# Scan loop of a fused MetaFormer kernel: PSUM places by first release, 14 slots, y summed five tiles behind the scan, GpSimd's u four tiles ahead, weighing by pairs of tiles

## What is computed

```python
def _mamba(x, in_w, conv_w, conv_b, x_w, dt_w, dt_b, A_log, D, out_w):
    ...
    xc = jax.nn.silu(jnp.transpose(xt, (0, 2, 1)))
    dbl = xc @ x_w.T
    dt, Bm, Cm = jnp.split(dbl, [DT_RANK, DT_RANK + D_STATE], axis=-1)
    dt = jax.nn.softplus(dt @ dt_w.T + dt_b)
    A = -jnp.exp(A_log)
    dA = jnp.exp(dt[..., None] * A)
    dBx = dt[..., None] * Bm[:, :, None, :] * xc[..., None]
    def step(h, inp):
        dA_t, dBx_t, C_t = inp
        h = dA_t * h + dBx_t
        y = jnp.einsum('bds,bs->bd', h, C_t)
        return (h, y)
    ...
    y = jnp.swapaxes(ys, 0, 1) + xc * D
    y = y * jax.nn.silu(z)
    return y @ out_w.T
```

## Time and profile before

| what | value |
|---|---|
| three runs | 901.69, 905.27, 906.05 us (median 905.27) |
| the profiled execution | 901.04 us, of which the span from first to last instruction is 899.3 us |
| scan loop, first POOL operation to last gate | 302.07 to 804.71 us |
| busy over the span | PE 708.9, DVE 721.3, POOL 516.2, ACT 369.3 us |
| DMA | 102.81 MB, 36.6% of the 16 engines for the main queue |

### The profile page before, as it was taken

One profiled execution on the slowest core, in us unless ns is written; L12 is line 12 of the kernel. 1 busy time (PEld: TensorE's weight loads), 2 busy tenths in 40 slices (PEclk: granted clock), 3 DMA queues, 4 the chain that ended last, 5 costly groups with the idle time before them and its releaser, 6 DMA issues. The chain is left out here.

```text
span 899.3 us, 19137 instructions
## 1 busy us (share of the span) xinstructions
PE 708.9 (79%) x7722; PEld 442.3 (49%) x7722; DVE 721.3 (80%) x938; ACT 369.3 (41%) x585; POOL 516.2 (57%) x407
## 2 busy tenths in 40 slices
PE   7987886699877387788878878887887787787696
PEld 3554553356554154544544544454454454446363
DVE  3998887763320489999999989999999999974998
ACT  2220002156536755545555555555455554321000
POOL 5000000000010489999999999999999999970043
PEclk9999998889989799999999999999999999998799
DMA  4000000000004256666666665666667666600001
GB/s 162 5 4 4 5 4 2 3 1 1 1 1 126 74 171 210 197 187 190 212 194 188 197 203 177 189 209 196 189 189 213 187 198 205 195 30 1 0 12 41
DMA packets 55866, 102.81 MB, mean 114 GB/s; under 512 B 11169, under 2 KB 13345, under 8 KB 55777
## 3 DMA queue, kind: packets, MB, share of 16 engines
q1 hardware_dynamic: 55552, 100.73, 36.6%
q0 software_dynamic: 224, 0.85, 0.2%
HBM read 98.00 MB, written 3.54 MB: 113 GB/s over the span
## 5 line engine op out<-in xcount | busy, mean ns | idle before, releaser
L546 POOL TENSOR_TENSOR ring<-ring,big 128x576 f32<-128x576 f32 x206 | 285.1, 1406 | 13.7 <-DVE ring L936 11.8
L184 PE MATMUL banks<-ring,main_params 128*128 128x288 f32 x824 | 244.2, 426 | 4.6 <-POOL ring L546 2.8
L936 DVE TENSOR_TENSOR_SCAN ring<-big,banks 128x576 f32<-128x576 f32 x154 | 202.6, 1340 | 2.3
L184 PEld LDWEIGHTS banks<-ring,main_params 128*128 128x128 f32 x824 | 146.4, 192 | 60.0 <-POOL ring L546 15.7
L924 DVE TENSOR_TENSOR banks<-banks,big 128x576 f32<-128x576 f32 x192 | 143.0, 745 | 24.0 <-PE banks L1218 21.4
L718 ACT ACTIVATE big<-big,small 128x576 f32<-128x576 f32 x192 | 142.2, 764 | 27.3 <-DVE ring L936 21.5
L523 POOL COPY big<-normed 128x288 f32<-128x288 f32 x8 | 3.0, 429 | 244.2 <-DVE normed L422 244.2
L1217 PE MATMUL banks<-big,selectors 96*128 96x512 bf16 x192 | 74.5, 390 | 80.0 <-DVE ring L936 37.4
L356 PE MATMUL banks<-big 32*32 32x288 f32 x3712 | 96.9, 429 | 21.3 <-issue 17.2
L790 DVE SCALAR_TENSOR_TENSOR big<-big 128x288 f32<-128x288 f32 x216 | 93.6, 512 | 0.0
L718 ACT ACTIVATE banks<-big,small 128x576 f32<-128x576 f32 x64 | 47.4, 741 | 108.2 <-DVE ring L936 86.9
(11 more groups left out here) (166 smaller groups left out, 962.5 us busy)
## 6 DMA issues: line engine op xcount, KB each, us to landing
big<-bc_rows SPq DMA_DIRECT2D x640, 144.0 KB, 3.2
bc_rows<-big SPq DMA_DIRECT2D x16, 144.0 KB, 2.4
residual<-x_in SPq DMA_DIRECT2D x2, 576.0 KB, 5.8
out<-big SPq DMA_DIRECT2D x2, 512.0 KB, 3.0
main_params<-main_in SPq DMA_DIRECT2D x1, 895.0 KB, 8.7
big<-front_in POOLq DMA_DIRECT2D x1, 574.5 KB, 5.7
experts<-experts_in SPq DMA_DIRECT2D x1, 512.0 KB, 9.0
row_selectors<-rows_in POOLq DMA_DIRECT2D x1, 256.0 KB, 5.9
```

The lines of the kernel that those rows point to most:

```text
L184: last = nc.tensor.matmul(PS[rows, 2 * p + a, 0:HALF], lhsT, rhs[:, bass.ds(at + a * HALF, HALF)], start=start, stop=stop, skip_group_chec ...
L546: nc.gpsimd.tensor_tensor(slot, slot, CT[n % 10], ALU.mult).then_inc(weighted, 1)
L936: nc.vector.tensor_tensor_scan(slot, DECAY[m % 3], place, 0.0, ALU.mult, ALU.add).then_inc(scanned, 1)
```

## The change

- A PSUM place goes to the user whose predecessor is released first by a small table of due times (`released`), instead of going round by three. bc stands behind tile 7 instead of 9.
- Two more pairs of slots, in the tensor XN, make 14 instead of 10. Slots come in pairs that lie side by side.
- POOL weighs two tiles in one operation of 1152 columns, and C is loaded for two tiles by one DMA per direction (five buffers of double width).
- POOL makes u four tiles ahead instead of two.
- PE adds y five tiles behind the scan instead of three, by a new list `ADDS`; the gate stands behind scan 5 instead of scan 3.
- A DVE multiply is put off by one tile where its place is released late (`late`), tiles 2, 8 and 9 instead of 2 and 10.

```diff
-        CT = [big(L) for _ in range(10)]
+        CT = [big(2 * L) for _ in range(5)]
...
-        MORE = [big(L) for _ in range(2)]
+        MORE = big(2 * L)
...
-        SLOT = [RING[:, i * L:(i + 1) * L] for i in range(8)] + MORE
+        SLOT_PAIR = ([RING[:, 2 * i * L:2 * (i + 1) * L] for i in range(4)] + [MORE] +
+                     [XN[:, 2 * i * L:2 * (i + 1) * L] for i in range(2)])
+        PAIRS = len(SLOT_PAIR)
+        SLOT = [t[:, i * L:(i + 1) * L] for t in SLOT_PAIR for i in range(2)]
...
-        V_AFTER, BC_AFTER = 1, 9
-        AHEAD = 2
+        V_AFTER, BC_AFTER = 1, 7
+        AHEAD, POOL_AHEAD = 2, 4
...
+        def released(user):
+
+            kind, i = user
+            if kind == "tile":
+                return i + 1
+            return (i - PREPARED) * DS + (V_AFTER if kind == "v" else BC_AFTER + 1.2)
+
+        HELD, PLACES, OWNER_AHEAD = [None] * 3, {}, {}
+        for user in USERS:
+            place = min(range(3), key=lambda p: -1 if HELD[p] is None else released(HELD[p]))
+            PLACES[user], OWNER_AHEAD[user] = place, HELD[place]
+            HELD[place] = user
...
+        def late(n):
+
+            owner = OWNER_AHEAD["tile", n]
+            return owner is not None and released(owner) > n - 1.4
...
-            for n in range(NTILES):
-                b, s = n // DS, n % DS
-                if s == 0:
-                    sp.wait_ge(rows_stored[b % 3], 16 * (b // 3 + 1))
-                if n >= 10:
-                    sp.wait_ge(weighted, n - 9)
-                spread_row(CT[n % 10], b, 1, s, c_loaded[n % 10])
...
+            for n in range(-POOL_AHEAD, NTILES):
+                m = n + POOL_AHEAD
+                if m < NTILES and m % DS == 0:
+                    sp.wait_ge(rows_stored[m // DS % 3], 16 * (m // DS // 3 + 1))
+                if m in POOL_TILES:
+                    load_b(m)
+                if n >= 0 and n % 2 == 0:
+                    load_c(n // 2)
...
-            def weigh(n):
-                pool.wait_ge(scanned, n + 1)
-                pool.wait_ge(c_loaded[n % 10], 32 * (n // 10 + 1))
-                slot = SLOT[n % SLOTS]
-                nc.gpsimd.tensor_tensor(slot, slot, CT[n % 10], ALU.mult).then_inc(weighted, 1)
+            def weigh(k):
+
+                pool.wait_ge(scanned, 2 * k + 2)
+                pool.wait_ge(c_loaded[k % 5], 32 * (k // 5 + 1))
+                slots = SLOT_PAIR[k % PAIRS]
+                nc.gpsimd.tensor_tensor(slots, slots, CT[k % 5], ALU.mult).then_inc(weighted, 1)
...
-            LATE = [V_AFTER + 1, BC_AFTER + 1]
             for n in range(-AHEAD, NTILES):
+                if n == 10:
+                    dve.wait_ge(z_mm, 2 * J)
                 if n >= 0:
                     scan(n)
                 for m in (n + 1, n + 2):
-                    if m in DVE_TILES and m - (1 if m % DS in LATE else 2) == n:
+                    if m in DVE_TILES and m - (1 if late(m) else 2) == n:
                         inputs_on_dve(m)
-                if n >= DS and n % DS == 3:
+                if n >= DS and n % DS == 5:
                     gate_image(n // DS - 1)
...
-                pe.wait_ge(weighted, n + 1)
+                pe.wait_ge(weighted, n // 2 + 1)
...
-            ADDS = [[-3], [-2], [-1], [], [0], [1, 2]] + [[s - 3] for s in range(6, DS)]
-            for n in range(-AHEAD, NTILES + 3):
+            ADDS = [[-5], [-4], [-3], [-2], [-1], [], [0], [1], [2, 3], [4]] + [[s - 5] for s in range(10, DS)]
+            for n in range(-AHEAD, NTILES + 5):
```

More of the change, by code:

```diff
@@ L220, in build_program @@
         rows_stored = [sem(f"rows_stored{i}") for i in range(3)]
-        c_loaded = [sem(f"c_loaded{i}") for i in range(10)]
+        c_loaded = [sem(f"c_loaded{i}") for i in range(5)]
         b_loaded = [sem(f"b_loaded{i}") for i in range(3)]
@@ L470, in store_rows, with spread_rows, load_b, load_c @@
                 sp.dma_start(BCD[b].rearrange("w d s t -> (w d s) t"), STAGE[b % 3]).then_inc(rows_stored[b % 3], 16)
[L472 removed]
+            def spread_rows(dst, b, w, s, count, loaded):
                 for d in range(2):
[L475 to L476 removed]
+                    rows = BCD[b, w, d, s:s + count].rearrange("s t -> (s t)")
+                    sp.dma_start(dst[d * DI:(d + 1) * DI, :], rows.unsqueeze(0).to_broadcast([DI, count * L])).then_inc(loaded, 16)
+            def load_b(n):
+                m = POOL_TILES.index(n)
+                if m >= 3:
+                    sp.wait_ge(u_pool, m - 2)
+                spread_rows(BT[m % 3], n // DS, 0, n % DS, 1, b_loaded[m % 3])
+            def load_c(k):
+                if k >= 5:
+                    sp.wait_ge(weighted, k - 4)
+                spread_rows(CT[k % 5], 2 * k // DS, 1, 2 * k % DS, 2, c_loaded[k % 5])
             for b in range(PREPARED):
                 store_rows(b)
[L480 to L493 removed]
+            for n in range(-POOL_AHEAD, NTILES):
[6 more added lines that the diff above has]
+                    load_c(n // 2)
+                if n >= 0 and n % DS == DS - 1 and n // DS + PREPARED < B:
+                    store_rows(n // DS + PREPARED)
             out_v = out.rearrange("(g p i) c -> p g (i c)", g=GROUPS, p=TOK)
@@ L540, in inputs_on_pool @@
                 nc.gpsimd.tensor_tensor(SLOT[n % SLOTS], BT[m % 3], DTX[n // DS % 2], ALU.mult).then_inc(u_pool, 1)
-            def weigh(n):
-                pool.wait_ge(scanned, n + 1)
-                pool.wait_ge(c_loaded[n % 10], 32 * (n // 10 + 1))
-                slot = SLOT[n % SLOTS]
-                nc.gpsimd.tensor_tensor(slot, slot, CT[n % 10], ALU.mult).then_inc(weighted, 1)
-            step_sizes(0)
-            for n in range(-AHEAD, NTILES + 1):
-                if n >= 1:
-                    weigh(n - 1)
-                if n + AHEAD in POOL_TILES:
-                    inputs_on_pool(n + AHEAD)
+            def weigh(k):
[3 more added lines that the diff above has]
+                nc.gpsimd.tensor_tensor(slots, slots, CT[k % 5], ALU.mult).then_inc(weighted, 1)
+            step_sizes(0)
+            for n in range(-POOL_AHEAD, NTILES + 1):
+                if n >= 2 and n % 2 == 0:
+                    weigh(n // 2 - 1)
+                if n + POOL_AHEAD in POOL_TILES:
+                    inputs_on_pool(n + POOL_AHEAD)
                 if n >= 0 and n % DS == 9 and n // DS + 1 < B:
```

7 lines of the change are left out of this document (3 added, 4 removed).

## The result

The changed kernel takes 922.3 us (median of four runs, 919.38 to 923.92), the kernel before 905.12 (four runs, 901.69 to 906.05). The ratio is 1.019, with a 95% interval from 1.016 to 1.023: slower by 1.9%, clear of the noise. The forecast was 910.8, its own range 904 to 920, the wide one 892 to 921; its sign was right and its size was not. The profiled execution took 919.38 us, its span is 917.6 us: 18.3 more than before.

The account below looks back on a forecast made before the run. DVE and POOL, nearly always busy, bound it, with DVE waiting on a PE and ACT chain. +0.9 - 2.0 + 0 + 10 - 2.0 = +6.9 on 901.04 gives 908; shifted to the runs, 910.8 us, range 904 to 920.

Parts of the forecast that it names:

- the term of the clock: PE's clock falling to 1.2 GHz around the gap before an image's y opening: +10 us, ends 0 and 25.
- Rival 3: PE's clock falls in every image at the full 1.7 us: 923 to 926 us; chance 0.07.
- The chain at tile 10: PE and ACT steps from the end of tile 6's scan to tile 10's multiply: 5.8 us, DVE waiting 1.9.
- The pair weighing: One POOL operation weighing two tiles takes 2.62 us against 2.81 for two; POOL stops being the bound.
- The end: After the last bc: 3.2 us given back, last scan to last gate 6.4 us instead of 5.2; together -2.0.
- The start: In image 0 the 2.18 us wait goes but the chain to tile 10 appears: 0, within 2 us.
- The first rival: PE's clock falls no more often than before: 898 to 900 us profiled, 900.7 to 903 on runs; chance 0.28.
- The second: In the loop bc's place is free in time, POOL sets the pace: 29.0 to 29.2 us an image; chance 0.17.

Follow-up runs that it names:

- five behind alone: Kernel before with only y summed five tiles behind the scan and the gate behind scan 5: 915.59 us, ratio 1.017.
- the gap filled: Changed kernel plus 18 small zero matmuls behind the last add of each image's y: 900.71 us, ratio 0.997 to the kernel before.
- the reordered kernel: Changed kernel plus 18 zero matmuls per image, y opening between take_high and take_middle, first adds behind tile 10's spread: 878.11 us, ratio 0.976 to kernel before.
- the zeros at the two ends changed: Kernel of 878.11 us without zeros behind the last image, with 8 zero matmuls in each of image 0's first seven turns: 874.88 us.
- the reordered one without zeros: Kernel of 878.11 us less its 18 zero matmuls per image: 942.91 us, ratio 1.043 to the kernel before.
- the places alone: Kernel before with only PSUM places by first release, bc behind tile 7 and put-off multiplies to match: 892.62 us, ratio 0.987.
- the pairs alone: Changed kernel with places round by three and y three behind again, leaving slots, pairs and u four ahead: 911.38 us, ratio 1.008 to kernel before.

## Why the prediction was wrong in size

The step that failed is the number of falls in the term of the clock. I took "a fall in 7 of 15 images at 1.4 us". The earlier trace rows shows the gap ahead of the one fall in fourteen images, 3 us that held one spread, and I made of the longer gap an even chance per image. It is no chance per image: each image has the same instructions at the same distances, and where falls are frequent they come in a fixed rhythm. With five behind alone they took two images in three, with the whole change all fifteen, and the two kinds of image alternated regularly. A count can't be interpolated between one in fourteen and all from one example. Rival 3, a fall in every image, was the case, at 0.07; its price of 1.7 us each was a little high.

The price was nearly right: 0.87 us for an image of 31.80 and 2.1 for one of 33.04, against 30.93 with the gap filled; 1.5 us on average, where I had 1.4. That is partly luck: I had 3.4 us at 1.2 GHz for each fall and at most 1.7 us of price, and every second fall lasted twice as long and cost more than that, while the others cost half of it. How it comes about is in the rows: the late spread of tile 9 costs 0.38 or 1.64 us (its multiply starts that much later than the 1.26 us of the scan ahead of it would have it), and the steps to the multiply of tile 10, 2.54 us apart with the clock held (446.35 to 448.89), are 3.03 apart (484.89 to 487.92). The whole chain, from the end of scan 6, is 6.75 us long in one kind of image (448.11 to 454.86) and 8.01 in the other (479.91 to 487.92), instead of 5.89. Thirteen images at 1.5 are 19.4 us in place of 10. That fills the gap between the forecast of 908 for the profiled time and the 919.38 measured, with 2 us over. The falls in the last two images account for about that: from gate to gate the last but one takes 29.63 us instead of 28.56, and the one behind it 23.11 where the kernel with the zeros, less the 1.7 us of zeros at its end, takes 22.3.

The other terms, with the clock held (the kernel with the gap filled):

- The chain at tile 10: 5.8 us predicted; the scan of tile 7 starts at 443.00 and the multiply of tile 10 at 448.89. The wait: 1.9 predicted, 1.9 measured (448.89 less 446.35 and 0.65 for the multiply). The image: 30.95 predicted, 30.93 to 30.94 measured.
- The pair weighing: 2.62 predicted, 2.626 measured. DVE does not wait for POOL in the scan of an image.
- The end: 6.4 us from the last scan to the last gate predicted; 816.59 to 823.00 is 6.41.
- The start: 0 within 2. The spans of the two kernels (897.4, which holds 1.7 us of zeros at the end, and 899.3) leave some -0.4 us for it.
- The first rival, "the clock does not fall more often", gave 898 to 900; with the zeros that time is reached, 899.19 in the profiled execution. The second, POOL or DVE at the pace of 29.0 to 29.2 us an image and some 873, did not come true for this order of instructions, and is what the reordered kernel does: 29.05 us an image, 878.11, and 874.88 with the zeros at the two ends changed.

The Trainium skill, page "Perfetto Trace Analysis", section Matmul Optimizations, says that the matmul engine scales its power with its utilization, so that it is important that matmuls execute back to back. The trace agrees, if the granted clock is taken for this scaling: the clock fell in every image both of the changed kernel and of the reordered one without zeros, at a price of some 20 us in the first and of 65 in the second. I had cited the rule and weighed it by how often it had acted in the kernel before, which was the wrong measure.

## What to carry to other kernels

Where PE is nearly idle for a moment in each turn of a loop and a chain that the bound engine waits for begins right behind it, look at the granted clock there; in a regular loop its falls can keep a rhythm (here four turns in six, two in three, or every turn, by the order of the work; where they were rare, no rhythm was seen), so a fall in every turn belongs well inside the range. Before moving matmuls, list for each gap what PE still does in it, and fill it with work that can move or with matmuls on zeros where a signal leaves room. Then look at the clock again, since zeros in one gap did not take away every fall in each order of the work. Two changes that each look free can need each other (pairs need y more than three tiles behind) or spoil each other (five tiles open the gap that the new places' chain starts from), so measure the parts alone: here the places alone gained 1.3% and the whole lost 1.9%.

## What the hardware did that I had not expected

- 18 matmuls of 224 columns, 1.9 us of PE an image, changed the time of the reordered kernel by 65 us (877.1 and 941.6 us of span), since without them 13.7 us of each image ran at 1.2 GHz.
- Frequent falls keep a fixed rhythm: images of 33.04 and 31.80 us alternate in the changed kernel, two images in three have a fall with five behind alone, and every image I measured in the kernel without zeros takes 34.14 us, with the fall at the same place. The rare ones (one image in the kernel before, three with the places alone, five with the pairs alone) do not show one.
- A fall costs by its length and by what waits behind it: with five behind alone an image with a fall costs 0.9 us, in the reordered kernel without zeros 5.1 us (34.14 against 29.05), because there it lasts 13.7 us and the multiplies of tiles 9, 10 and 12 wait.
